# Decoder of two layers: the attention line of head pairs, with PSUM dealt anew between maxima and scores

## Chip, cores and metric

The program runs on one core of one Trainium2 chip, as one launch. The metric is the device time of an execution in microseconds (us), lower is better.

## What is computed

The reference is a decoder of two layers on x of 8 x 256 tokens by 128 features, with a context of the same size. Each of its six sublayers is followed by a layer norm of the sum with its input. Five stages of the kernel are attention with 16 heads of 8 features; what they share, cut to the core:

```python
q, k, v = split_heads(x @ Wq.T), split_heads(x @ Wk.T), split_heads(x @ Wv.T)
scores = einsum('bhqd,bhkd->bhqk', q, k) / sqrt(8)      # + a bias or a mask, by stage
attn = softmax(scores, axis=-1)
out = einsum('bhqk,bhkd->bhqd', attn, v)                # then out @ Wo.T in three of them
x = _layernorm(x + out)
```

The stages in order: **a0**, self-attention with rotary positions, 8 batches of 256 x 256 scores; **x0**, causal attention to the context with a linear bias; **f0**, causal attention among tokens that a router selects, 4 pairs of batches of 128 x 128 scores; **a1**, self-attention with a learned Gaussian bias, 8 batches; **x1**, attention to the context under an integer mask, 8 batches. Between them lie projections, layer norms, a gated layer after f0, and at the end a top-2 mixture of eight experts.

## The kernel before

It is written in Bass: each engine (PE = TensorE, DVE = VectorE, ACT = ScalarE, POOL = GpSimd, SP for the DMA queue) has its own instruction stream, and semaphores join them. No scheduler moves anything.

`Core` (tensor, scalar, vector, gpsimd, sync) is one attention stage. A batch, or a pair of selected batches in f0, is an **item**. Its 16 heads are 8 **pairs** u = 0..7, one head in rows 0 to 63 of the arrays Q6 and K6, the other in rows 64 to 127. Queries and keys stand there as six bf16 parts of each fp32 number. Each head is computed twice:

- **Maxima** (L413): queries on the partitions, 62 rows of contraction. DVE takes the negated row maxima from PSUM into MS (L574). After four pairs, a **half**, POOL splits them in two bf16 parts (L639, L640), PE turns them (L466, `turn_m`), ACT copies them to MT (L537), and SP writes them by DMA into rows 62, 63 and 126, 127 of Q6 (L684), against rows of ones in K6.
- **Scores** (L420): keys on the partitions, 64 rows of contraction, so that the row maximum is already subtracted. ACT takes the exponential from PSUM into PT (L550), and PE multiplies it with the values and a column of ones, in fp32, four heads side by side in 32 columns each (L480, `values`: one call for four heads, a **group**). ACT copies the result to OT (L529, `evacuate`), PE turns it (L493, `turn_context`), DVE divides by the sum (L589, L590, `context`).

Where a stage has a bias that is no extra row (x0, f0, x1), one more matmul with the identity adds it to each bank of maxima and of scores (L429).

PSUM has eight banks of 2 KB a partition. Before: banks 0 to 3 hold scores, two banks a pair and two pairs in turn; bank 4 holds the maxima of one head of the pair and bank 5 those of the other; bank 6 the products with the values; bank 7 what is turned.

`steps` walks j = 0..nb+1: in turn j the maxima are those of item j (`bm`), the scores those of item j-1 (`be`), and the end of item j-2 (`bc`) follows. Within a turn, `heads` gives for each pair u two phases a = 0, 1: in a phase the maxima of head a and the scores of head 1-a alternate matmul by matmul, so that two run side by side in the two halves of the rows. Only item j's maxima run in the first turn, so the scores follow eight pairs behind.

```python
if bm:
    after(pe, self.mx_done, H * bm.no + 2 * u + a - 1)
```

is the wait of a phase for the maxima bank, and `after(pe, self.exp_done, be.no * 8 + u - 1)` the wait for the score banks. `Post` puts pieces of the next projection and layer norm (T, C, P, A, M, N) into the last two turns, at the places in PLACES.

Of the kernel before, what the change touches and what calls it, by code (L numbers as in the profile page):

```python
# [333 lines left out]
class Item:  # L334
# [3 lines left out]
    def __init__(self, core, no, feat):  # L338
        self.core, self.no = core, no
        self.par = no % 2  # L340
        self.buf, self.use = no % NBUF, no // NBUF
        self.feat = feat


class Core:
# [3 lines left out]
    def __init__(self, g, nb, nqt, causal=False, bias=None, extra=None, xrows=0):  # L349
        assert nb % NBUF == 0  # L350
# [6 lines left out]
        self.tail = None  # L357

        self.st_ready = g.shared_sem("core_st_ready", 8 * nb)
        self.exp_done = g.shared_sem("core_exp_done", 8 * nb)  # L360
        self.mx_ready = g.shared_sem("core_mx_ready", H * nb)
        self.mx_done = g.shared_sem("core_mx_done", H * nb)
        self.mb_ready = g.shared_sem("core_mb_ready", 2 * nb)
        self.mt_ready = g.shared_sem("core_mt_ready", 2 * nb)
        self.mts_done = g.shared_sem("core_mts_done", 2 * nb)
        self.pv_done = g.shared_sem("core_pv_done", 4 * nb)
        self.ot_done = g.shared_sem("core_ot_done", 4 * nb)
        self.va_ready = g.shared_sem("core_va_ready", nb)
        self.cxt_ready = g.shared_sem("core_cxt_ready", nqt * nb)
        self.cx_done = g.shared_sem("core_cx_done", nqt * nb)  # L370
        self.chain = g.shared_sem("core_chain", nqt * nb)
        self.m_chain = g.shared_sem("core_m_chain", 2 * nb)
        self.joined = g.shared_sem("core_joined", 2 * nb if causal else 0)
        self.feat = [g.shared_sem(f"core_feat{i}", 16 * sum(self.loads(n) for n in range(i, nb, NBUF))) for i in range(NBUF)]
        self.m_in = [[g.shared_sem(f"core_m_in{i}{h}", 32 * nb // NBUF) for h in range(2)] for i in range(NBUF)]
        self.items = []
        for n in range(nb):
            loads = sum(self.loads(i) for i in range(n % NBUF, n + 1, NBUF))
            self.items.append(Item(self, n, 16 * loads))
# [1968 lines left out]
```

## Time and profile before

| | us |
|---|---|
| median of 3 executions | 1121.19 |
| lowest, highest | 1118.40, 1122.68 |
| the profiled execution | 1118.82 |
| its span, first to last instruction | 1117.0 |
| PE busy | 823.5 (74%) |
| DVE busy | 628.2 (56%) |
| ACT busy | 519.7 (47%) |
| mean granted TensorE clock | 0.823 |

The profiled execution takes 1.8 us more than its span. A busy PE is pipelined and its ends are modelled, so its share says little; the stages have different limits, and each is read by itself. The attention lines run from about 62 to 193 (a0), 220 to 360 (x0), 424 to 486 (f0), 572 to 704 (a1) and 731 to 911 us (x1); the experts follow to the end. A granted clock of 1.00 is 2.4 GHz, one of 0.50 is 1.2 GHz.

### The profile page before, as it was taken

To read this page: it belongs to the slowest core of one execution; us is meant where nothing else is said; L and a number is where in the kernel's file an instruction comes from. 1 tells how busy PE (TensorE), PEld (TensorE's weight loads), DVE (VectorE), ACT (ScalarE), POOL (GpSimd) and SP (SyncE) were. 2 spreads that over 40 slices of the span, in tenths; PEclk is the share of its full clock that TensorE was granted. 3 is DMA by queue.
4 is the path that set the end of the run, shared out by engine and by line. 5 is a ranking of instruction groups with operands and counts; after the bars stand their busy time and mean duration, and the time that the engine had idled before them with its cause. 6 is when DMAs were issued, how large, how long until landed. Compare 5 with 4: busy or idle time off the path is not lost.

```text
span 1117.0 us, 20492 instructions
## 1 busy us (share of the span) xinstructions
PE 823.5 (74%) x7236; PEld 457.0 (41%) x7237; DVE 628.2 (56%) x1590; ACT 519.7 (47%) x867; POOL 182.3 (16%) x312
## 2 busy tenths in 40 slices
PE   6167777489997546965847777489999962999970
PEld 3013334224443332433513334213333442999970
DVE  3287774466674733326257774446666435555567
ACT  2237776435555321313617776405555531666630
POOL 3421110100110020000501110210000006403214
PEclk9659999569998765558759999759999975999985
DMA  5842205332101022000522210142120051212212
GB/s 160 230 131 64 59 6 170 96 95 59 57 5 72 28 61 70 2 1 4 168 58 64 64 34 2 40 114 63 31 58 2 2 226 45 74 48 67 66 39 70
DMA packets 75657, 75.56 MB, mean 68 GB/s; under 512 B 21473, under 2 KB 65249, under 8 KB 74801
## 3 DMA queue, kind: packets, MB, share of 16 engines
q1 hardware_dynamic: 72400, 64.10, 20.9%
q0 software_dynamic: 3168, 10.29, 2.8%
q8 instruction: 55, 0.90, 0.4%
q14 instruction: 34, 0.27, 0.1%
HBM read 50.66 MB, written 23.13 MB: 66 GB/s over the span
## 4 chain that ended last, share of the span: by engine, by line
PE 61%; DVE 14%; issue 7%; SPq 5%; DMA 5%; POOL 4%; ACT 4%; POOLq 0%; ACTq 0%; DVEq 0%
PE PS L413 12%; PE PS L429 12%; PE PS L480 11%; PE PS L1611 7%; DVE MS L574 7%; PE PS L493 4%; PE PS L1621 3%; SPq L666 3%; PE PS L420 2%; PE PS L827 1%; PE PS L173 1%; POOL experts_x L1522 1%; ACT X L858 1%; DMA rows_k<-parts 1%; DMA BIG<-MT 1%
## 5 line engine op out<-in xcount | busy, mean ns | idle before, releaser
L574 DVE TENSOR_REDUCE MS<-PS 128x2 f32<-128x512 f32 (+2 forms) x576 | 341.2, 615 | 163.3 <-PE PS L429 120.5
L550 ACT ACTIVATE BIG<-PS 128x1024 f32<-128x1024 f32 (+2 forms) x288 | 259.9, 906 | 218.7 <-PE PS L429 157.2
L413 PE MATMUL PS<-BIG 62*128 62x256 bf16 (+1 forms) x1088 | 216.5, 287 | 131.0 <-DVE MS L574 56.6
L420 PE MATMUL PS<-BIG 64*128 64x256 bf16 (+1 forms) x1088 | 198.2, 274 | 0.5 <-DMA BIG<-MT 0.5
L413 PEld LDWEIGHTS PS<-BIG 62*128 62x128 bf16 x1088 | 70.3, 96 | 280.9 <-issue 189.0
L480 PE MATMUL PS<-BIG,VA 128*32 128x256 f32 (+1 forms) x2176 | 143.7, 377 | 3.5 <-ACT OT L529 3.5
L1611 PE MATMUL PS<-OT,VA 128*128 128x128 f32 x736 | 96.2, 278 | 0.4 <-ACT OT L1668 0.4
L1611 PEld LDWEIGHTS PS<-OT,VA 128*128 128x128 f32 x736 | 91.0, 195 | 0.6 <-ACT OT L1668 0.6
L480 PEld LDWEIGHTS PS<-BIG,VA 128*32 128x32 f32 x2176 | 62.4, 111 | 50.9 <-issue 29.9
L639 POOL CAST MB<-MS 128x16 bf16<-128x16 f32 (+1 forms) x72 | 14.1, 196 | 413.7 <-DVE MS L574 323.6
L589 DVE RECIPROCAL rsum<-PS 128x16 f32<-128x16 f32 x68 | 17.5, 257 | 110.3 <-PE PS L493 110.3
L300 POOL TENSOR_TENSOR parts<-rbuf,parts 128x512 bf16<-128x512 f32 x34 | 40.0, 1185 | 226.9 <-ACT parts L225 226.8
L420 PEld LDWEIGHTS PS<-BIG 64*128 64x128 bf16 x1088 | 66.9, 95 | 11.8 <-issue 5.5
L1663 ACT COPY VA<-BIG 128x1024 f32 x46 | 48.1, 1046 | 42.0 <-PE PS L1611 40.6
L1702 DVE SCALAR_TENSOR_TENSOR turn<-fbuf,PS 128x512 f32<-128x512 f32 x46 | 31.6, 687 | 55.4 <-ACT fbuf L1678 55.4
L537 ACT COPY MT<-PS 16x256 bf16<-16x256 bf16 (+1 forms) x72 | 24.5, 341 | 80.8 <-PE PS L466 65.9
L529 ACT COPY OT<-PS 128x256 f32<-128x256 f32 (+1 forms) x144 | 51.1, 355 | 16.3 <-PE PS L480 16.1
L493 PE MATMUL PS<-ident,OT 128*128 128x128 f32 x272 | 47.1, 299 | 15.7 <-issue 12.9
L429 PE MATMUL PS<-mask_q,ident_bf 128*128 128x512 bf16 x128 | 53.8, 421 | 0.0
L871 PE MATMUL PS<-ident,X 128*128 128x128 f32 x80 | 20.1, 401 | 40.5 <-ACT X L858 35.0
L1621 PE MATMUL PS<-BIG,rbuf 128*128 x368 | 49.1, 276 | 0.8 <-DVE Y L1716 0.8
L429 PE MATMUL PS<-mask_k,ident_bf 128*128 128x512 bf16 x128 | 49.2, 384 | 0.0
(218 smaller groups left out, 1092.3 us busy)
## 6 DMA issues: line engine op xcount, KB each, us to landing
rows_q<-parts SPq DMA_DIRECT2D x32, 192.0 KB, 2.3
rows_k<-parts SPq DMA_DIRECT2D x32, 192.0 KB, 2.2
BIG<-rows_q SPq DMA_DIRECT2D x64, 96.0 KB
BIG<-rows_k SPq DMA_DIRECT2D x64, 96.0 KB
BIG<-in_ex_w SPq DMA_DIRECT2D x3, 2048.0 KB, 12.0
BIG<-rows_q SPq DMA_DIRECT2D x64, 64.0 KB
BIG<-rows_k SPq DMA_DIRECT2D x64, 64.0 KB
OT<-experts_x SPq DMA_DIRECT2D x46, 64.0 KB, 1.8
```

The costliest lines, as they stand in the source:

```text
L300: nc.gpsimd.tensor_tensor(self.part(m, 2), g.rbuf[m % 2][:, :], self.part(m, 1), ALU.subtract).then_inc(self.s3_ready.sem, 1)
L413: return nc.tensor.matmul(g.bank[4 + a][:, first:first + kw], g.Q6[b.buf][rows, u, qt * P:(qt + 1) * P], g.K6[b.buf][rows, u, 0:kw], start ...
L420: return nc.tensor.matmul(g.bank[2 * (u % 2) + a][:, self.offset[kt]:self.offset[kt] + n], g.K6[b.buf][rows, u, kt * P:(kt + 1) * P], g.Q6 ...
L429: return nc.tensor.matmul(self.biased(bank), g.ident_bf[:, :], bias, start=False, stop=True)
L480: last = nc.tensor.matmul(g.bank[6][PVW * hh:PVW * hh + PVW, lo:lo + n], g.VA[b.par][:, kt, 8 * (hh % 2) + 2 * grp + hh // 2, :], g.PT[grp ...
L493: last = nc.tensor.transpose(g.bank[7][:, grp * P:(grp + 1) * P], g.OT[b.par][:, grp, qt * P:(qt + 1) * P], g.ident[:, :])
L529: nc.scalar.copy(g.OT[b.par][:, grp, 0:w], g.bank[6][:, 0:w])\
L550: nc.scalar.activation(g.PT[grp % 2][:, 2 * (u % 2):2 * (u % 2) + 2, 0:self.width], g.bank2[u % 2][:, :, 0:self.width], ACT.Exp, scale=SCALE)\
L574: nc.vector.tensor_reduce(g.MS[:, 0:n, a, u], g.bank[4 + a][:, 0:n * w].rearrange("p (n k) -> p n k", n=n), axis=AX_X, op=ALU.max, negate= ...
L1611: last = nc.tensor.matmul(g.bank[2 * a + b.par][:, f * P:(f + 1) * P], self.wb[b.par][:, a, f * P:(f + 1) * P], self.xt[b.par], start=True ...
L1621: last = nc.tensor.matmul(g.bank[6][:, 0:D], self.hid[b.par][:, f * P:(f + 1) * P], self.w3[:, bass.ds(e, 1), f, :].rearrange("p e d -> p ...
L1663: nc.scalar.copy(self.wb[b.par], self.w12[:, :, bass.ds(self.expert(nc.scalar, b), 1), :] .rearrange("p a e f -> p a (e f)"))
```

## The change

A class `Line` takes over the five engine streams from `Core`, with one count of steps for all stages. A step is one pair: maxima of pair `step`, scores of pair `step - LAG`, and LAG is 10.

- PSUM: banks 0 and 1 hold the scores, one for each head of the pair; banks 2 to 5 the maxima, two banks a pair and two pairs in turn. Banks 6 and 7 stay.
- Maxima: one reduction over both banks of a pair (288 instructions in place of 576), and one semaphore step a pair. A pair waits for the reduction two pairs before.
- Scores: one exponential a head (576 in place of 288), one semaphore step a head. A head's scores wait for the exponential of the same head of the pair before.
- `values` of a group comes in two parts, kt = 0 and kt = 1, each between the two phases of a step: kt = 0 at odd, kt = 1 at even score pairs. `turn_context` comes in two halves of two transposes each, in two steps.
- `evacuate` and the exponentials stand in this order in a step of ACT. On SP, the six key loads of an item stand after the maxima rows of the item two before, the query loads ahead of them. `Post`'s places are steps after the last maxima: the moments (M0) now stand at step 4.
- The semaphores are no longer per stage. The matmuls, their operands and the copies are the same.

The core of the diff:

```diff
+        for step in range(8 * first, 8 * end + self.TAIL):
+            yield step, inside(step, 8), inside(step - self.LAG, 8)
...
+        k, n = divmod(step - self.LAG - 14, 8)
+        b = self.item(items, k)
+        qt, half = {0: (0, 0), 1: (0, 1), 3: (1, 0), 4: (1, 1)}.get(n, (2, 0))
+        return (b, qt, half) if b and qt < b.core.nqt else (None, 0, 0)
...
+        k, n = divmod(step - 2, 8)
+        return (self.item(items, k - 1), 1) if n == 0 else (self.item(items, k), 0) if n == 4 else (None, 0)
...
-            return nc.tensor.matmul(g.bank[4 + a][:, first:first + kw], g.Q6[b.buf][rows, u, qt * P:(qt + 1) * P],
...
+            return nc.tensor.matmul(g.bank[2 + 2 * (u % 2) + a][:, first:first + kw], g.Q6[b.buf][rows, u, qt * P:(qt + 1) * P],
...
-            return nc.tensor.matmul(g.bank[2 * (u % 2) + a][:, self.offset[kt]:self.offset[kt] + n],
...
+            return nc.tensor.matmul(g.bank[a][:, core.offset[kt]:core.offset[kt] + n],
...
-        def phase(bm, be, u, a):
-
-            if bm:
-                after(pe, self.mx_done, H * bm.no + 2 * u + a - 1)
-            for i in range(nqt):
...
+        def phase(step, bm, be, a):
+
+            u, v = step % 8, (step - self.LAG) % 8
+            if bm and a == 0:
+                after(pe, self.mx_done, step - 1)
+            if be:
+                after(pe, self.exp_done, 2 * (step - self.LAG) + a - 1)
+            for i in range(2):
+                if bm and i < bm.core.nqt:
+                    mx = maxima(bm, u, a, bm.core.nqt - 1 - i, bm.core.bias is None or i == 0)
+                if be and i < be.core.nqt:
+                    st = scores(be, v, 1 - a, i, be.core.bias is None or i == 0)
...
+            if bm and a == 1:
                 mx.then_inc(self.mx_ready.sem, 1)
-            if be and a == 1:
+            if be:
                 st.then_inc(self.st_ready.sem, 1)
...
+            b, grp = self.group(items, n), n % 4
...
+                pe.wait_ge(*self.exp_done.at(4 * n + 4))
+            lo, w = core.queries[kt]
+            for hh in range(4):
+                last = nc.tensor.matmul(
+                    g.bank[6][PVW * hh:PVW * hh + PVW, lo:lo + w],
+                    g.VA[b.par][:, kt, 8 * (hh % 2) + 2 * grp + hh // 2, :],
+                    g.PT[grp % 2][:, hh, core.offset[kt]:core.offset[kt] + w],
+                    start=kt == 0, stop=kt == core.nqt - 1)
+            if kt == core.nqt - 1:
+                last.then_inc(self.pv_done.sem, 1)
...
+            if half == 0:
...
+            for grp in (2 * half, 2 * half + 1):
+                last = nc.tensor.transpose(g.bank[7][:, grp * P:(grp + 1) * P], g.OT[b.par][:, grp, qt * P:(qt + 1) * P],
+                                           g.ident[:, :])
+            if half == 1:
+                last.then_inc(self.cxt_ready.sem, 1)
+                self.bank7_read = self.cx_done.at(b.cx + qt + 1)
...
+        for step, bm, be in self.steps(items):
...
+            phase(step, bm, be, 0)
+            grp, kt = divmod(step - self.LAG - 3, 2)
+            values(grp, kt)
+            phase(step, bm, be, 1)
+            b, half = self.maxima_of(items, step)
+            if b:
+                turn_m(b, half)
+            b, qt, half = self.turns_of(items, step)
+            if b:
+                turn_context(b, qt, half)
+            if tail:
+                tail.run("tensor", pe, step)
+
...
-        def evacuate(b, grp):
-            act.wait_ge(*self.pv_done.at(b.no * 4 + grp + 1))
...
+            act.wait_ge(*self.pv_done.at(n + 1))
...
+            nc.scalar.copy(g.OT[b.par][:, grp, 0:w], g.bank[6][:, 0:w]).then_inc(self.ot_done.sem, 1)
...
+        def exponential(b, v):
+            if v % 2 == 0:
+                after(act, self.pv_done, v // 2 - 1)
+            w = b.core.width
+            for n, a in enumerate((1, 0)):
+                act.wait_ge(*self.st_ready.at(2 * v + n + 1))
+                nc.scalar.activation(g.PT[v // 2 % 2][:, 2 * (v % 2) + a, 0:w], g.bank[a][:, 0:w], ACT.Exp, scale=SCALE)\
+                  .then_inc(self.exp_done.sem, 1)
...
+            if v % 2 == 0:
+                evacuate(v // 2 - 2)
+            if be:
+                exponential(be, v)
...
-            n, w = self.mx_blocks, P if self.causal else nqt * P
-            for a in range(2):
-                dve.wait_ge(*self.mx_ready.at(H * b.no + 2 * u + a + 1))
-                nc.vector.tensor_reduce(g.MS[:, 0:n, a, u], g.bank[4 + a][:, 0:n * w].rearrange("p (n k) -> p n k", n=n),
-                                        axis=AX_X, op=ALU.max, negate=True).then_inc(self.mx_done.sem, 1)
+            dve.wait_ge(*self.mx_ready.at(step + 1))
+            nc.vector.tensor_reduce(g.MS[:, 0:n, :, u].rearrange("p n a -> p a n"),
+                                    g.bank2[1 + u % 2][:, :, 0:n * w].rearrange("p a (n k) -> p a n k", n=n),
+                                    axis=AX_X, op=ALU.max, negate=True).then_inc(self.mx_done.sem, 1)
...
+        for step, bm, be in self.steps(items):
+            if bm:
+                maxima(bm, step)
+                if bm.core.causal and step % 4 == 3:
+                    join(bm, step % 8 // 4)
+            b, qt, half = self.turns_of(items, step)
+            if b and half == 1:
+                context(b, qt)
+            if tail:
...
+        for b in items:
+            parts_of_m(b, 0)
+            value_rows(b)
+            parts_of_m(b, 1)
...
+    def sync(self, sp, items, rows):
...
+        for step, bm, be in self.steps(items):
+            b, half = self.maxima_of(items, step)
+            if b:
+                m_rows(b, half)
+            k, n = divmod(step, 8)
+            if n == 4:
+                b = self.item(items, k + 2)
+                if b:
+                    self.load(sp, b, rows, "qx")
+            if n == 0 and k > items[0].k:
+                b = self.item(items, k + 1)
+                if b:
+                    self.load(sp, b, rows, "k")
...
-    PLACES = {(0, 0): "T0 C0", (0, 1): "P0 T1 C1", (0, 2): "A0 P1 T2 C2", (0, 3): "A1 P2 M0", (1, 0): "A2", (1, 3): "N0 N1",
+    PLACES = {0: "T0 C0", 1: "P0 T1 C1", 2: "A0 P1", 4: "A1 M0", 5: "T2 C2", 6: "P2", 7: "A2", 12: "N0 N1",
...
-        self.bank2 = [PS[:, 2 * i:2 * i + 2, :] for i in range(2)]
+        self.bank2 = [PS[:, 2 * i:2 * i + 2, :] for i in range(3)]
```

The order on **PE** in a0, before: the second phase of pair 3, then a whole group of values and a whole context (L413 maxima, L420 scores, L480 values, L493 contexts).

```order
L413 MATMUL PS<-BIG 128x256 [waits core_mx_done]
L420 MATMUL PS<-BIG 128x256
L413 MATMUL PS<-BIG 128x256
L420 MATMUL PS<-BIG 128x256
L480 MATMUL PS<-BIG,VA 32x256 [waits core_ot_done,core_exp_done]
L480 MATMUL PS<-BIG,VA 32x256 x7
L493 MATMUL PS<-ident,OT 128x128 [waits core_ot_done,core_cx_done,core_mts_done]
L493 MATMUL PS<-ident,OT 128x128 x3
```

The same place in the changed kernel, one step of an odd score pair (L461 maxima, L468 scores, L525 values, L540 contexts): the first phase, half a group of values, the second phase, half a context.

```order
L461 MATMUL PS<-BIG 128x256 [waits core_exp_done,core_mx_done]
L468 MATMUL PS<-BIG 128x256
L461 MATMUL PS<-BIG 128x256
L468 MATMUL PS<-BIG 128x256
L525 MATMUL PS<-BIG,VA 32x256 [waits core_ot_done,core_exp_done]
L525 MATMUL PS<-BIG,VA 32x256 x3
L461 MATMUL PS<-BIG 128x256 [waits core_exp_done]
L468 MATMUL PS<-BIG 128x256
L461 MATMUL PS<-BIG 128x256
L468 MATMUL PS<-BIG 128x256
L540 MATMUL PS<-ident,OT 128x128 x2
```

The values and the context are cut in two, and half of the values stands between the phases. In an even step that half is kt = 1, whose last matmul is what `core_pv_done` counts.

The order on **ACT** in a0, before: a group's copy (L529), two exponentials of two heads each (L550), the copy of turned maxima (L537).

```order
L529 COPY OT<-PS 128x256 [waits core_cxt_ready,core_pv_done]
L550 ACTIVATE BIG<-PS 128x1024 [waits core_pv_done,core_st_ready]
L550 ACTIVATE BIG<-PS 128x1024 [waits core_st_ready]
L537 COPY MT<-PS 16x256 [waits core_m_in30,core_mt_ready]
L529 COPY OT<-PS 128x256 [waits core_pv_done]
```

The changed kernel at this place: the copy (L578), the two exponentials of an even pair (L586), the copy of turned maxima (L595), the two of an odd pair, the next copy.

```order
L578 COPY OT<-PS 128x256 [waits core_cxt_ready,core_pv_done]
L586 ACTIVATE BIG<-PS 128x512 [waits core_st_ready,core_pv_done]
L586 ACTIVATE BIG<-PS 128x512 [waits core_st_ready]
L595 COPY MT<-PS 16x256 [waits core_m_in30,core_mt_ready]
L586 ACTIVATE BIG<-PS 128x512 [waits core_st_ready] x2
L578 COPY OT<-PS 128x256 [waits core_pv_done]
```

Twice as many exponentials of half the width stand there, and the copy at the head of an even step waits for the half of values that PE issues in the same step.

## Rows read from the trace of the kernel before

**Rows 1.** Stretches: length, busy us (x) of PE, PEld, DVE, ACT, POOL, PEclk, DMA share, GB/s.

```profile
93.40:149.68 56.28, 42.65 (x564) 20.53 (x560) 44.31 (x80) 39.87 (x57) 5.77 (x20) 1.00 0.24 58
258.27:331.27 73.00, 71.53 (x865) 33.09 (x861) 51.32 (x110) 41.76 (x71) 7.22 (x25) 1.00 0.15 44
731.47:749.03 17.56, 17.56 (x50) 3.81 (x50) 10.39 (x15) 0.36 (x1) 0.42 (x2) 0.50 0.56 131
776.19:871.92 95.73, 95.73 (x864) 32.62 (x860) 61.75 (x100) 50.28 (x71) 7.20 (x25) 1.00 0.12 33
452.86:465.14 12.28, 12.28 (x110) 5.50 (x102) 5.15 (x18) 4.41 (x15) 1.17 (x6) 0.50 0.01 2
```

**Rows 2.** Timeline of x1, PE: start us, us, engine line op out<-in xcount [idle <-releaser].

```profile
757.56 1.07 PE L480 MATMUL PS<-BIG,VA 128*32 128x256 f32 x16
758.57 0.28 PE L413 MATMUL PS<-BIG 62*128 62x256 bf16 x1
...
759.43 0.28 PE L413 MATMUL PS<-BIG 62*128 62x256 bf16 x1
...
762.02 1.07 PE L480 MATMUL PS<-BIG,VA 128*32 128x256 f32 x16
762.90 0.28 PE L466 MATMUL PS<-ident_bf,MB 128*16 128x128 bf16 x2
```

**Rows 3.** Timeline of x0, PE.

```profile
242.46 0.28 PE L413 MATMUL PS<-BIG 62*128 62x256 bf16 x1
...
243.06 0.86 PE L480 MATMUL PS<-BIG,VA 128*32 128x256 f32 x16
```

**Rows 4.** Timeline of a0, PE.

```profile
110.07 0.28 PE L413 MATMUL PS<-BIG 62*128 62x256 bf16 x1
...
110.39 1.07 PE L480 MATMUL PS<-BIG,VA 128*32 128x256 f32 x16
...
113.58 1.07 PE L480 MATMUL PS<-BIG,VA 128*32 128x256 f32 x16
114.58 0.66 PE L493 MATMUL PS<-ident,OT 128*128 128x128 f32 x4
...
115.17 0.28 PE L413 MATMUL PS<-BIG 62*128 62x256 bf16 x1
```

**Rows 5.** Timeline of a0, ACT and DVE.

```profile
110.53 1.02 ACT L550 ACTIVATE BIG<-PS 128x1024 f32<-128x1024 f32 x1 [0.70 <-PE PS L420]
...
111.86 0.36 ACT L529 COPY OT<-PS 128x256 f32<-128x256 f32 x1
111.91 2.54 DVE L574 TENSOR_REDUCE MS<-PS 128x2 f32<-128x512 f32 x4 [0.65 <-PE PS L413]
...
112.17 1.02 ACT L550 ACTIVATE BIG<-PS 128x1024 f32<-128x1024 f32 x1
...
114.72 0.37 ACT L529 COPY OT<-PS 128x256 f32<-128x256 f32 x1
```

**Rows 6.** Groups by line and shape: busy us, mean ns | idle us before <-releaser.

```profile
L574 DVE TENSOR_REDUCE MS<-PS 128x2 f32<-128x512 f32 x384 | 251.4, 688 | 86.3 <-PE PS L429 48.5 <-PE PS L413 34.0 <-POOL MB L640 0.6
...
L550 ACT ACTIVATE BIG<-PS 128x768 f32<-128x768 f32 x64 | 51.8, 810 | 54.6 <-PE PS L429 54.6
...
L1678 ACT ACTIVATE fbuf<-PS 128x512 f32<-128x512 f32 x46 | 27.4, 597 | 6.2 <-PE PS L1611 3.2
```

**Rows 7.** Timeline after the last maxima of a0.

```profile
178.67 0.38 ACT L529 COPY OT<-PS 128x256 f32<-128x256 f32 x1
...
179.19 1.07 PE L480 MATMUL PS<-BIG,VA 128*32 128x256 f32 x16 [0.49 <-ACT OT L529]
```

**Rows 8.** Timeline, PE: the first scores of x0.

```profile
236.46 0.37 PE L413 MATMUL PS<-BIG 62*128 62x256 bf16 x1 [3.72 <-DMA BIG<-MT]
```

**Rows 9.** Timeline, PE: the first scores of f0.

```profile
435.44 0.26 PE L413 MATMUL PS<-BIG 62*128 62x128 bf16 x1 [4.02 <-DMA BIG<-MT]
```

**Rows 10.** Timeline, PE: the last context of x0.

```profile
359.13 1.09 PE L493 MATMUL PS<-ident,OT 128*128 128x128 f32 x4 [5.22 <-issue]
```

More of the change, by code:

```diff
@@ L356, in __init__ @@
         self.mx_blocks = 3 if causal else nqt
[L357 to L379, printed above, removed]
+        self.items = g.line.add(self)
     def loads(self, no):
         return 12 + (2 if self.xrows else 0) + (2 if self.extra is not None and no < NBUF else 0)
-    def steps(self, body):
-        for j in range(self.nb + 2):
-            body(j, *(self.items[j - lag] if 0 <= j - lag < self.nb else None for lag in range(3)))
     def bias_for(self, b, transposed):
@@ L416, in scores @@
[L416 to L422 removed]
+            core, rows = b.core, slice(64 * a, 64 * a + MROW)
+            first = P if core.causal and qt == 1 else qt * core.nqt * P
@@ L446, in phase, with turn_m @@
                 mx.then_inc(self.mx_ready.sem, 1)
-            if be and a == 1:
+            if be:
                 st.then_inc(self.st_ready.sem, 1)
-        def heads(bm, be, u):
-            if bm and u == 0:
+        def turn_m(b, half):
+            pe.wait_ge(*self.mb_ready.at(2 * b.k + half + 1))
+            if self.bank7_read:
+                pe.wait_ge(*self.bank7_read)
+            for qt in range(b.core.nqt):
+                last = nc.tensor.transpose(g.aux_bf[0:16, qt * P:(qt + 1) * P], g.MB[half][:, qt, :], g.ident_bf[:, :])
+            last.then_inc(self.mt_ready.sem, 1)
+            self.bank7_read = self.mts_done.at(2 * b.k + half + 1)
@@ L453, in heads @@
+        self.bank7_read = None
+        for step, bm, be in self.steps(items):
+            if bm and step % 8 == 0:
                 pe.wait_ge(*self.feat[bm.buf].at(bm.feat))
             if be:
-                if u % 4 == 0:
-                    pe.wait_ge(*self.m_in[be.buf][u // 4].at((be.use + 1) * 32))
-                after(pe, self.exp_done, be.no * 8 + u - 1)
-            phase(bm, be, u, 0)
-            phase(bm, be, u, 1)
-        def turn_m(b, half):
-            after(pe, self.cx_done, self.turned)
-            pe.wait_ge(*self.mb_ready.at(b.no * 2 + half + 1))
-            for qt in range(nqt):
-                last = nc.tensor.transpose(g.aux_bf[0:16, qt * P:(qt + 1) * P], g.MB[half][:, qt, :], g.ident_bf[:, :])
-            last.then_inc(self.mt_ready.sem, 1)
-            self.m_turned += 1
@@ L487, in turn_context @@
-        def turn_context(b, qt):
-            after(pe, self.mts_done, self.m_turned)
-            after(pe, self.cx_done, self.turned)
-            pe.wait_ge(*self.ot_done.at(b.no * 4 + 4))
-            for grp in range(4):
-                last = nc.tensor.transpose(g.bank[7][:, grp * P:(grp + 1) * P], g.OT[b.par][:, grp, qt * P:(qt + 1) * P],
-                                           g.ident[:, :])
-            last.then_inc(self.cxt_ready.sem, 1)
-            self.turned += 1
-        self.m_turned = self.turned = 0
@@ L780, in run @@
         if place != "after":
-            place = (place[0] - self.core.nb, place[1])
+            place -= 8 * self.core.items[-1].k + 8
         pieces = {"T": self.turn, "C": self.copy, "P": self.project, "A": self.add,
```

409 lines of the change are left out of this document (193 added, 216 removed).

## Prediction

> **What bounds the kernel now.** I read first the windows over whole items of each stage [rows 1], since the page's shares are means over stages with different limits. In a0 an item takes 56.28 / 4 = 14.07 us; PE is busy 42.65 of the 56.28 and DVE 44.31, so none is full, and a ring of waits sets the pace. a1 has the same pitch. In x0 an item takes 73.00 / 5 = 14.60 us and in x1 95.73 / 5 = 19.15 us, and there PE is busy 71.53 of 73.00 and all of the stretch. f0 takes 12.28 us an item at a granted clock of 0.50, PE busy throughout. Then the timelines, for which ring it is in a0: DVE reduces four banks in 2.54 us, idle 0.65 us before them for a PE matmul [rows 5], and PE's phases wait for the maxima bank just reduced. That wait, at every phase, is what four banks of maxima take away. Last, the edges: x0's and f0's first scores stood 3.72 and 4.02 us for the maxima rows' DMA [rows 8, 9], and x0's last context waited 5.22 us with no releaser named, behind DVE's moments [rows 10].
>
> **What takes its place.** With two banks of scores, phase 0 of a step must wait for the exponential of that head in the step before; with half of the values between the phases, an even step's exponentials stand behind a copy that waits for the values of the same step. So a double step is a chain through PE, ACT and back. Its parts:
> - Values on PE: sixteen matmuls are followed by a maxima matmul after 1.01 us and by a transpose after 0.88 us [rows 2], so a half is 0.44 us, and the change to a phase 0.13 us more: 0.57 us.
> - Phase: 0.32 us in a0 [rows 4], 0.60 in x0 [rows 3], 0.86 in x1 [rows 2].
> - Start of the values to the copy's start: 1.14 us for a group (113.58 to 114.72) [rows 4, 5], less 0.44: 0.70.
> - Copy to exponential: 111.86 to 112.17 is 0.31 us; phase start to exponential is 0.46 us (110.07 to 110.53) [rows 4, 5].
> - Exponential of 512 columns: no row has it from PSUM to PT. 1024 columns take 1.02 us [rows 5], 768 take 0.81 and an ACT read of 512 elsewhere takes 0.597 [rows 6]; the two lines give 0.60, and 0.49 for 384. Bounds: half of 1.02 (0.51) and 0.81.
> - End of an ACT instruction to PE's start: 178.67 + 0.38 to 179.19 is about 0.11 us with the rounding [rows 7].
> - Context: 0.59 us for four transposes [rows 4], so 0.37 for two, if about 0.15 of it is the change of operands and comes again. Bounds 0.30 and 0.59.
>
> **a0 and a1.** Even step: 0.32 + 0.70 + 0.31 + 0.60 + 0.11 = 2.04 us. Odd step: 0.46 + 0.60 + 0.11 = 1.17, or 1.55 in the two that carry half a context. An item: 4 x 2.04 + 2 x 1.17 + 2 x 1.55, plus 0.3 for ACT's two copies of turned maxima, is 13.9 us against 14.07: the ring of DVE goes, and one of nearly the same length comes. With LAG 10, 54 of 64 steps carry both kinds of work (before 56), that is 6.75 items: -0.8 us. Edges: ten maxima steps in place of eight, bound by DVE. The merged reduction has no row: two single ones are 1.38 us [rows 6], four in a row go at 2.54 / 4 = 0.635 a piece, so 1.27 a pair [rows 5]; I take 1.2, between 1.07 (0.69 and half of 0.76) and 1.38. So 12.0 - 11.0 = +1.0, two full steps of 1.76 less, -3.5, and two more score steps without maxima at the mean of the chain, 2 x 1.6 = +3.2. Each stage: -0.1 us.
>
> **x1.** PE has no idle time, so each added piece counts. Values per item: eight halves at 0.57 = 4.60 for four groups of 0.88 to 1.00, together 3.76: +0.84. Contexts: 4 x 0.37 for 2 x 0.59: +0.3. The chain of an even step, 0.86 + 0.70 + 0.31 + 0.60 + 0.11 = 2.58, is 0.08 longer than PE's own work in the two steps with turned maxima: +0.16. Together +1.3, by 6.75 items +8.9 us. Edges: a maxima step at the low clock is 17.56 / 8 = 2.19 us [rows 1]; two of these and two score steps of 1.6 for two full ones of 2.39: +2.8. Sum +11.7.
>
> **x0.** Even step 0.60 + 0.49 + 0.31 + 0.49 + 0.11 = 2.00 (values and exponential of the narrower causal form), odd step 0.60 + 0.57 + 0.60 = 1.77 on PE, twice with 0.37: 15.8 us against 14.60, by 6.75 +8.3 us. Edges: the maxima rows now stand ahead of the key loads on SP, and the wait of 3.72 [rows 8] covers two more maxima steps of 1.38, which leaves -0.96; two full steps less, -3.65; two score steps more, +3.5, less about half of the 5.22 [rows 10], since the moments now stand at step 4, which leaves +1.0 of the score steps. Sum +4.7.
>
> **f0.** Only one key block, so kt = 1 is empty and no half is added; the split contexts and exponentials add about 0.4 an item at half clock: +1.1. The wait of 4.02 [rows 9] covers two more maxima steps of at most an eighth of an item, 12.28 / 8 = 1.54, and leaves -0.9; two full steps less: -3.1; two score steps of about 1.2, an estimate from 1.54 less the maxima: +2.4. Sum -0.5.
>
> **POOL, SP, DVE.** POOL's parts and SP's DMAs are as many as before. DVE issues 288 instructions fewer, which is worth nothing once it isn't the ring; the 0.65 us gap [rows 5] covers it, and if the chain above were shorter than DVE's 1.2 a step it would count.
>
> **Sum.** -0.1 - 0.1 + 11.7 + 4.7 - 0.5 = +15.7 us on the profiled 1118.82, 1134.5; the median of the runs is 2.4 us higher, so about **1136 us**. Its own range, from the bounds of the exponential (two of them in the chain of a double step: 0.09 us less each takes 4 x 2 x 0.09 x 6.75 = 4.9 us from a0 and as much from a1), and of the context (0.59 in place of 0.37 adds 4 x 0.22 x 6.75 = 5.9 us in x1 and as much in x0, where PE is full): 1125 to 1146.
>
> **A rule against this change.** The rows show 0.13 us between values and a phase where the next matmul reads other rows [rows 2], and the sum uses that. The Trainium skill, "TensorEngine Tiling (Array Packing)", section "Key Properties", says that a change of the tiling mode drains TensorE, and values in four tiles of 32 columns between phases in two row halves are such changes, now twice as many; the trace agrees that there is a price. Sixteen values matmuls take 1.07 us to their last end [rows 2] and the next one of a phase starts 0.06 us before that; taking the whole pipeline, an estimate by that rule, 0.2 us for each of the eight halves in place of 0.13 would add some 0.6 us an item in x1 and 2 to 4 us in all.
>
> **Rivals.**
> - **The chain does not bind (faster).** Place: ACT's copy at the head of an even step in a0 and a1. If the values' half ends so early beside the phases that the exponential starts with its scores, a double step falls to what DVE needs, 2 x 1.2 + its share of divisions, 2.75 us instead of 3.5, an item to 11.0: (14.07 - 11.0) x 13.5 = -41 us, about 1095; half way is about 1115. It decides at a double step under 3.4 us. For it: PE and DVE are each idle a quarter of the stretch [rows 1]. Against: 0.70 and 0.31 are rows of instructions that stay. The Trainium skill, "VectorE: DVE Perf Modes", section "The DRAIN you can't avoid", states that a DVE instruction starts only when the one before has emptied the pipe, which would favour one instruction a pair; the row of four at 0.635 apiece where one takes 0.69 shows little such gap here. Chance 0.14.
> - **Splitting costs nothing on PE (no change).** If values and contexts in halves run as fast as whole, and x0's chain hides behind PE, the 8.9 and 8.3 us go: about 1119. For it: transposes follow values in 0.88. Against: 1.01 where a phase follows. Chance 0.19.
> - **Late maxima rows (slower still).** Scores wait for the DMA that SP issues. If each half of an item comes some 0.5 us late in 27 items of the four long stages, that is +25 us, about 1161. For it: [rows 8, 9] show such waits at the edges. Against: LAG 10 gives two steps, over 3 us, more. Chance 0.15.
> - Forecast: 0.52.
>
> **Numbers.** The range leaves out the far ends of the first and third rivals: 1110 to 1156. A measurement here tells some 0.5%, 5.6 us, from no change, 1115.6 to 1126.8. Faster: the first rival and a little of the second, 0.18. Same: the rest of the second and the forecast's low end, 0.22. Slower: 0.60.
>
> **What would show it.** Windows of 14.0 us an item in a0 and a1, 15.8 in x0, 20.5 in x1, 12.7 in f0. One group of 288 reductions, about 1.2 us at full width. In even steps ACT's copies wait for PE's values and PE's phases for ACT; DVE's idle time grows. The clock stays. A double step in a0 under 3.4 us, or x1 still at 19.2 an item, would make it wrong.

## The result, and the profile after

The changed kernel takes 1122.86 us (median of 20 executions), the kernel before 1119.53 (20 executions): a ratio of 1.0034, 95% interval 1.0017 to 1.005. That is a small loss, a fifth of the one forecast (about 16 us), and inside the 0.5% that the prediction called no change. The profiled execution's span grew from 1117.0 to 1118.7 us.

Busy time by engine, from the page of the changed kernel, and its costliest groups on DVE, ACT and PE:

```profile
PE 855.2 (76%) x7236; PEld 436.8 (39%) x7237; DVE 595.9 (53%) x1302; ACT 545.7 (49%) x1155; POOL 181.3 (16%) x312
...
L619 DVE TENSOR_REDUCE MS<-PS 128x4 f32<-128x1024 f32 (+2 forms) x288 | 307.7, 1076 | 236.2 <-PE PS L478 180.7
L586 ACT ACTIVATE BIG<-PS 128x512 f32<-128x512 f32 (+2 forms) x576 | 298.5, 540 | 147.1 <-PE PS L478 112.5
L461 PE MATMUL PS<-BIG 62*128 62x256 bf16 (+1 forms) x1088 | 213.9, 291 | 109.1 <-ACT BIG L586 25.9
```

DVE has 288 instructions less and 32 us less work, ACT 288 more and 26 us more, and PE, with the same 7236 matmuls, 32 us more busy time. PE's phases now wait for the exponential (L461, 25.9 us in all).

The windows of the changed kernel, two items of a0, x0 and x1, one of f0, and the ten maxima steps at the start of x1 (columns as in [rows 1]):

```profile
106.50:133.97 27.47, 23.84 (x282) 8.57 (x281) 21.31 (x25) 20.90 (x45) 2.77 (x10) 1.00 0.21 60
270.92:301.86 30.94, 29.61 (x345) 12.41 (x344) 18.16 (x28) 17.92 (x45) 2.78 (x10) 1.00 0.19 54
799.12:839.02 39.90, 39.85 (x345) 12.67 (x344) 21.76 (x25) 21.97 (x45) 2.90 (x10) 1.00 0.14 42
450.18:462.58 12.40, 12.40 (x104) 5.39 (x103) 4.04 (x10) 5.43 (x22) 1.12 (x5) 0.50 0.01 3
726.62:748.51 21.89, 21.89 (x64) 4.74 (x64) 11.03 (x9) 0.36 (x1) 1.38 (x5) 0.50 0.38 104
```

An item takes 13.73 us in a0 (and a1), 15.47 in x0, 19.95 in x1 and 12.40 in f0. Before it was 14.07, 14.60, 19.15 and 12.28 by [rows 1]. The windows here run from one transpose of maxima to that of an item later; taken so, the full items before come out at the same 14.07, 14.60 and 19.15.

The new chain can be read off the timelines of PE and ACT in a0 (matmuls of maxima, values, context):

```profile
107.33 0.27 PE L461 MATMUL PS<-BIG 62*128 62x256 bf16 x1 [0.55 <-ACT BIG L586]
...
108.53 0.27 PE L461 MATMUL PS<-BIG 62*128 62x256 bf16 x1
...
108.85 0.64 PE L525 MATMUL PS<-BIG,VA 128*32 128x256 f32 x8
...
109.42 0.28 PE L461 MATMUL PS<-BIG 62*128 62x256 bf16 x1
...
110.58 0.27 PE L461 MATMUL PS<-BIG 62*128 62x256 bf16 x1 [0.39 <-ACT BIG L586]
...
112.17 0.28 PE L461 MATMUL PS<-BIG 62*128 62x256 bf16 x1
```

```profile
109.56 0.37 ACT L578 COPY OT<-PS 128x256 f32<-128x256 f32 x1 [0.28 <-PE PS L525]
109.83 1.77 ACT L586 ACTIVATE BIG<-PS 128x512 f32<-128x512 f32 x3
```

An even step runs from 108.53 to 110.58: phase 0.32, values to the copy's start 0.71, copy to exponential 0.27, exponential and the way back 0.75. That is 2.05 us where the prediction summed 2.04. The odd step without a context runs from 107.33 to 108.53, 1.20 us (predicted 1.17), the one with a context from 110.58 to 112.17, 1.59 (predicted 1.55). But neither at 108.53 nor at 112.17 does PE wait: these steps are as long as PE's own work (0.32 + 0.57 + 0.31 is 1.20), and not as long as a chain through ACT, so that their sums came out close by luck. Four even steps, two odd ones and two with a context make 13.78 of the measured 13.73 us; the 0.3 that the prediction added for ACT's copies of turned maxima isn't there.

The table shows where the 1.7 us between the profiled spans come from, by part of a stage, beside the prediction's terms. "Full" runs from the first scores to the last maxima, "fill" is before it, "drain" after it to the end of the last context:

| us | fill: before, after, change (forecast) | full | drain | stage (forecast) |
|---|---|---|---|---|
| a0 | 25.03, 24.52, -0.5 (+1.0) | 96.29, 91.05, -5.2 (-4.3) | 22.70, 26.02, +3.3 (+3.2) | -2.4 (-0.1) |
| x0 | 16.32, 15.50, -0.8 (-1.0) | 100.81, 103.05, +2.2 (+4.6) | 22.94, 23.47, +0.5 (+1.0) | +1.9 (+4.7) |
| f0 | 11.52, 10.59, -0.9 (-0.9) | 35.48, 31.63, -3.9 (-2.0) | 14.34, 16.71, +2.4 (+2.4) | -2.4 (-0.5) |
| a1 | 11.56, 11.10, -0.5 (+1.0) | 96.46, 93.00, -3.5 (-4.3) | 23.26, 26.47, +3.2 (+3.2) | -0.7 (-0.1) |
| x1 | 17.57, 21.89, +4.3 (+4.4) | 131.08, 132.26, +1.2 (+4.1) | 29.27, 31.99, +2.7 (+3.2) | +8.2 (+11.7) |

With -2.9 us between the stages and at both ends (forecast 0) this is +1.7 (forecast +15.7). No single term was off by more than 3 us.

### The profile page after: what moved, and what is told of

Read it like the earlier page. It is cut to its first block, busy times and chain, and to the rows that moved or that the text cites. A ratio compares the mean times of both kernels' runs of the same rounds, so it can differ in the third digit from the quotient of the medians.

```text
span 1118.7 us, 20452 instructions
## 1 busy us (share of the span) xinstructions
PE 855.2 (76%) x7236; PEld 436.8 (39%) x7237; DVE 595.9 (53%) x1302; ACT 545.7 (49%) x1155; POOL 181.3 (16%) x312
## 4 chain that ended last, share of the span: by engine, by line
PE 62%; DVE 11%; ACT 8%; issue 7%; POOL 4%; DMA 4%; SPq 3%; POOLq 0%; ACTq 0%; DVEq 0%
PE PS L525 13%; PE PS L461 12%; PE PS L478 12%; PE PS L1653 7%; ACT BIG L586 4%; PE PS L1663 3%; PE PS L468 3%; DVE MS L619 3%; PE PS L540 2%; SPq L707 2%; PE PS L173 1%; POOL experts_x L1564 1%; PE PS L869 1%; ACT X L900 1%; DMA rows_k<-parts 1%
## 5 line engine op out<-in xcount | busy, mean ns | idle before, releaser
L619 DVE TENSOR_REDUCE MS<-PS 128x4 f32<-128x1024 f32 (+2 forms) x288 | 307.7, 1076 | 236.2 <-PE PS L478 180.7
L586 ACT ACTIVATE BIG<-PS 128x512 f32<-128x512 f32 (+2 forms) x576 | 298.5, 540 | 147.1 <-PE PS L478 112.5
L461 PE MATMUL PS<-BIG 62*128 62x256 bf16 (+1 forms) x1088 | 213.9, 291 | 109.1 <-ACT BIG L586 25.9
L468 PE MATMUL PS<-BIG 64*128 64x256 bf16 (+1 forms) x1088 | 211.0, 275 | 2.6 <-ACT BIG L586 2.4
L461 PEld LDWEIGHTS PS<-BIG 62*128 62x128 bf16 x1088 | 66.4, 97 | 272.0 <-issue 189.5
L525 PE MATMUL PS<-BIG,VA 128*32 128x256 f32 (+1 forms) x2176 | 169.5, 385 | 2.5 <-ACT OT L578 2.5
L578 ACT COPY OT<-PS 128x256 f32<-128x256 f32 (+1 forms) x144 | 51.9, 360 | 78.8 <-PE PS L525 78.6
L468 PEld LDWEIGHTS PS<-BIG 64*128 64x128 bf16 x1088 | 64.5, 96 | 30.1 <-issue 15.3
L525 PEld LDWEIGHTS PS<-BIG,VA 128*32 128x32 f32 x2176 | 43.9, 110 | 71.1 <-issue 54.6
L595 ACT COPY MT<-PS 16x256 bf16<-16x256 bf16 (+1 forms) x72 | 24.2, 336 | 81.3 <-PE PS L507 66.2
L540 PE MATMUL PS<-ident,OT 128*128 128x128 f32 x272 | 57.0, 299 | 7.2 <-DVE CX L637 6.8
```

Of the source, the lines that this page charges most:

```text
L461: return nc.tensor.matmul(g.bank[2 + 2 * (u % 2) + a][:, first:first + kw], g.Q6[b.buf][rows, u, qt * P:(qt + 1) * P], g.K6[b.buf][rows, u ...
L468: return nc.tensor.matmul(g.bank[a][:, core.offset[kt]:core.offset[kt] + n], g.K6[b.buf][rows, v, kt * P:(kt + 1) * P], g.Q6[b.buf][rows, ...
L525: last = nc.tensor.matmul(g.bank[6][PVW * hh:PVW * hh + PVW, lo:lo + w], g.VA[b.par][:, kt, 8 * (hh % 2) + 2 * grp + hh // 2, :], g.PT[grp ...
L540: last = nc.tensor.transpose(g.bank[7][:, grp * P:(grp + 1) * P], g.OT[b.par][:, grp, qt * P:(qt + 1) * P], g.ident[:, :])
L578: nc.scalar.copy(g.OT[b.par][:, grp, 0:w], g.bank[6][:, 0:w]).then_inc(self.ot_done.sem, 1)
L586: nc.scalar.activation(g.PT[v // 2 % 2][:, 2 * (v % 2) + a, 0:w], g.bank[a][:, 0:w], ACT.Exp, scale=SCALE)\
```

## The experiments

Each is an edit of the changed kernel, beside which the before-kernel ran on the same chip. The ratio is to the kernel before; "against the change" compares medians with its 1122.86.

### Where the values stand: whole_odd, whole_even

```diff
-            if not b or kt >= b.core.nqt:
+            if not b or kt != min(0, b.core.nqt - 1):     (whole_even: min(1, ...))
                 return
...
-            lo, w = core.queries[kt]
-            for hh in range(4):
+            for kt in range(core.nqt):
+                lo, w = core.queries[kt]
+                for hh in range(4):
```

> The values of a group are not split: all eight matmuls (both key blocks) stand between the phases of the odd step, where the first half stood. Chain theory (an even step's copy and exponentials wait for the values half that PE issues in the same step): in a0 and a1 that wait goes, but the odd step gets longer, a double step about 3.35 us in place of 3.43, an item 13.4 in place of 13.73; in x1 PE does four groups of 1.0 instead of eight halves of 0.57, an item 19.3 in place of 19.95; x0 15.1 in place of 15.47. In all about -12 us against the changed kernel. Rival (the two score banks alone set the pace, the copy's place is nothing): a0 and a1 gain nothing or lose 0.4 an item, in all about -4 to 0.

> All of a group's values stand between the phases of the even step, where the second half stood. Chain theory: the chain of the even step grows by the first half, 0.44 us: a0 and a1 13.73 + 4 x 0.43 = 15.4 us an item, x0 16.7, x1 19.7 (PE saves 0.6, the chain takes 0.3 back); about +30 us against the changed kernel. Rival (the copy's place is nothing): the same work as the run before, so the same time, -4 to 0 us.

whole_odd took 1105.86 us, ratio 0.9877 (0.9827 to 0.9926), -17 us against the change; whole_even 1128.95, ratio 1.0087 (1.0056 to 1.0117), +6 us. Windows of two items of a0, x0, x1, first of whole_odd, then of whole_even:

```profile
108.01:135.58 27.57, 22.85 (x283) 9.54 (x281) 21.04 (x25) 20.44 (x45) 2.78 (x10) 1.00 0.21 60
270.93:299.60 28.67, 28.29 (x345) 13.03 (x344) 17.91 (x29) 18.55 (x45) 2.78 (x10) 1.00 0.19 58
...
789.71:827.90 38.19, 37.24 (x339) 13.26 (x345) 21.76 (x25) 22.17 (x44) 2.77 (x10) 1.00 0.15 44
```

```profile
111.03:140.34 29.31, 23.85 (x283) 9.46 (x281) 21.41 (x24) 19.96 (x45) 2.90 (x10) 1.00 0.19 56
280.45:310.88 30.43, 28.79 (x346) 13.35 (x345) 18.17 (x29) 17.89 (x45) 2.90 (x10) 1.00 0.19 55
...
810.55:849.37 38.82, 37.80 (x340) 13.49 (x345) 21.77 (x25) 21.96 (x45) 2.90 (x10) 1.00 0.14 43
```

The two hold the same instructions; only the place differs, and with it a0's item is 13.78 or 14.65 us, x0's 14.34 or 15.22, x1's 19.10 or 19.41. So the rival by which the copy's place is nothing falls. PE's timeline of whole_even shows the longer chain, its even step going from 120.38 to 122.86, 2.48 us, which is 2.05 and the other half's 0.43:

```profile
120.38 0.27 PE L461 MATMUL PS<-BIG 62*128 62x256 bf16 x1
...
120.71 1.07 PE L525 MATMUL PS<-BIG,VA 128*32 128x256 f32 x16
...
122.86 0.27 PE L461 MATMUL PS<-BIG 62*128 62x256 bf16 x1 [0.39 <-ACT BIG L585]
```

Its item grew by 0.92 us, not the 1.7 expected: four such double steps of 2.48 and about 1.18 us are the 14.65. That is less than expected, since two of the four double steps carried half a context in the odd step and had taken 3.63 us already; in whole_even that context hides in the longer wait. In whole_odd a0 kept its time (13.4 was expected): the odd step is longer by the same half, and once an item the transposes of maxima stand for DVE's context, 0.86 us where the changed kernel has 0.39:

```profile
115.53 0.27 PE L507 MATMUL PS<-ident_bf,MB 128*16 128x128 bf16 x2 [0.86 <-DVE CX L636]
```

x0 and x1 gained more than expected, and x1 is back at its pace before the change. So in x1 all of the +0.80 us an item, and in x0 more than all of the +0.87, hangs on the split and on where the second half stands.

### Two reductions a pair: two_red

```diff
-            nc.vector.tensor_reduce(g.MS[:, 0:n, :, u].rearrange("p n a -> p a n"),
...
+            for a in range(2):
+                last = nc.vector.tensor_reduce(g.MS[:, 0:n, a, u],
...
+            last.then_inc(self.mx_done.sem, 1)
```

> The banks stay as changed, but DVE reduces a pair in two instructions of one head each, with one semaphore step after the second. Chain theory: DVE is off the path in full steps, items stay at 13.7, 15.5 and 19.95; only the ten maxima steps at a stage's start run at 1.3 to 1.4 us in place of 1.2, +1 to +2 us in each of a0, x0 and a1, in all +3 to +6 us. Rival (DVE still sets the pace in a0 and a1, so the merged reduction is what the change gains by): 0.15 us a step and more, +10 us in each of a0 and a1, +20 us in all.

1122.01 us, ratio 1.0027 (0.9997 to 1.0057), -1 us against the change; items 13.73, 15.48 and 19.96 as there. The merged reduction is worth nothing that can be told in this kernel.

### The lag: lag9

```diff
-    LAG = 10
+    LAG = 9
```

The turned contexts keep their steps.

> The scores follow nine pairs behind the maxima instead of ten (the turned contexts stay at their absolute steps). If LAG 10 pays for the way of the maxima rows: from the transpose to the second DMA's issue is 2.2 us in the changed kernel's trace, and with some 2 us to land about 4.2 us; two steps between cover 3.4 in a0 and a1, so PE waits 0.8 us twice an item there, 15.3 in place of 13.73, and little in x0 and x1; about +15 to +25 us less 4 for the edges. Rival (two steps cover it, as in the kernel before): items as now, each stage one maxima step and one score step shorter at its edges and one full step longer, -3 to -5 us in all.

1131.75 us, ratio 1.0099 (1.0078 to 1.0119), +9 us against the change. Items 14.21, 15.89 and 20.37, each 0.42 to 0.48 longer. But inside the full steps PE never waits for the maxima rows' DMA; only first scores do, those of f0 for 2.69 us, against 1.54 with LAG 10 and 4.02 before [rows 9], those of a0 and a1 for 1.01 and 0.85, against nothing. So both expectations miss. In a0 the timeline shows the reason: with an odd LAG the transposes of maxima fall in odd score steps, where nothing hides them, and the double step with them takes 126.26 - 122.78 = 3.48 us in place of 3.25:

```profile
122.78 0.27 PE L461 MATMUL PS<-BIG 62*128 62x256 bf16 x1 [0.76 <-ACT BIG L586]
...
124.00 0.28 PE L507 MATMUL PS<-ident_bf,MB 128*16 128x128 bf16 x2
...
126.26 0.27 PE L461 MATMUL PS<-BIG 62*128 62x256 bf16 x1 [0.76 <-ACT BIG L586]
```

In x0 and x1 it is PE's wait for exponentials that grew: over two items each of lag9's trace it stands 2.2 us (x0) and 0.9 (x1) in front of L461, against 1.3 and nothing in the changed kernel, that is 0.4 us an item in both. An even step keeps the length of its chain when the transposes leave it, and the odd step gets longer by them.

### Whole contexts: ctx_whole

```diff
-            for grp in (2 * half, 2 * half + 1):
+            if half == 0: return
+            for grp in range(4):
```

> Contexts are turned whole (four transposes in the step of the second half). The prediction priced the split at +0.3 us an item, so by it x1 falls from 19.95 to 19.65 and x0 from 15.47 to 15.2, -4 us in all. Rival (the split of a context costs nothing, since the two switches are no dearer than one phase's end that overlaps them): all items as now, 0 +- 1 us; in a0 and a1 the DVE's context comes at the same step in both cases.

1118.23 us, ratio 0.9981 (0.996 to 1.0003), -5 us against the change. But x0 stayed at 15.48 and x1 rose to 20.10, while a0 and a1 fell to 13.56. The term it tests, +0.3 us an item for the split in the stages where PE is full, has the wrong sign in x1. The timelines say what a context costs PE there. From the start of the phase before it to the next phase, first in the changed kernel (half a context), then in ctx_whole (a whole one):

```profile
810.82 0.28 PE L461 MATMUL PS<-BIG 62*128 62x256 bf16 x1
...
811.58 0.38 PE L540 MATMUL PS<-ident,OT 128*128 128x128 f32 x2
811.90 0.28 PE L461 MATMUL PS<-BIG 62*128 62x256 bf16 x1
```

```profile
810.41 0.28 PE L461 MATMUL PS<-BIG 62*128 62x256 bf16 x1
...
811.18 0.60 PE L541 MATMUL PS<-ident,OT 128*128 128x128 f32 x4
811.71 0.28 PE L461 MATMUL PS<-BIG 62*128 62x256 bf16 x1
```

The half takes 1.08 us and the whole 1.30; less a phase of 0.86 that is 0.22 for two transposes and 0.44 for four, so in x1 the split of a context costs PE nothing. And two of the four halves of an item fall in even steps, whose length of 2.58 us is the chain's. With whole contexts one even step has none, and waits for its exponential all the same:

```profile
821.47 0.27 PE L461 MATMUL PS<-BIG 62*128 62x256 bf16 x1 [0.22 <-ACT BIG L587]
```

### One exponential a pair: one_exp

```diff
-            for n, a in enumerate((1, 0)):
-                act.wait_ge(*self.st_ready.at(2 * v + n + 1))
...
+            act.wait_ge(*self.st_ready.at(2 * v + 2))
+            nc.scalar.activation(g.PT[v // 2 % 2][:, 2 * (v % 2):2 * (v % 2) + 2, 0:w], g.bank2[0][:, :, 0:w], ACT.Exp, scale=SCALE)\
```

> The exponential of a pair is one instruction over both score banks (1024 columns), as before the change, with the banks as changed. Chain theory: each step becomes a chain through both phases and the whole exponential: a0 and a1 0.89 + 0.46 + 1.02 + 0.11 = 2.48 us a step, 19.8 an item; x0 about 2.8 a step, 22.6 an item; x1 3.5 a step, 28 an item; about +190 us against the changed kernel. Rival (ACT and PE overlap otherwise, the split of the exponential only costs instructions): ACT saves 0.1 us a pair, no change or a few us less.

1531.62 us (one execution), +409 us against the change: the chain is there, and in all it costs twice the 190 us expected. Windows of two items of a0 and of x1:

```profile
140.35:195.81 55.46, 40.78 (x282) 10.63 (x280) 21.75 (x24) 20.32 (x28) 2.88 (x10) 0.50 0.10 30
...
1165.50:1223.74 58.24, 39.46 (x340) 12.90 (x345) 21.76 (x25) 20.31 (x28) 2.89 (x10) 1.00 0.10 29
```

In x1, at a granted clock of 1.00, an item takes 29.1 us where the chain gave 28. In a0 it takes 27.7 where the chain gave 19.8, and there the granted clock has fallen to 0.50. So the split of the exponential is what makes two banks of scores bearable.

### Values one step early: early, early_mixed

```diff
-            grp, kt = divmod(step - self.LAG - 3, 2)
+            grp, kt = divmod(step - self.LAG - 2, 2)
...
             for n, a in enumerate((1, 0)):
+                if v % 2 == 1 and n == 1:
+                    evacuate((v - 3) // 2)
...
-            if v % 2 == 0:
-                evacuate(v // 2 - 2)
```

The copy now stands between the two exponentials of the odd step. early_mixed adds: in x0 and x1 both halves at the odd step.

> The halves stay, one step earlier (first half in the even step right after the group's exponentials, second half in the odd step), and ACT's copy stands between the two exponentials of the odd step, so that no exponential waits for values of its own step. Chain theory: a double step in a0 and a1 becomes 0.89 + 1.17 + 0.89 = 2.95 us, an item 12.0 to 12.3 in place of 13.73; x0 15.3, x1 19.8; about -23 us against the changed kernel. Rival (ACT's load or the two score banks set the pace): a0 and a1 stay at 13.7, total within 5 us of the changed kernel.

> As the run with the values one step early and ACT's copy between the exponentials, and in x0 and x1, where PE is full, the values of a group whole in the odd step. a0 and a1 13.2 as in that run; x0 14.3 in place of 14.64, x1 19.1 in place of 19.65; -6 us against that run, about 1093. Rival (the split costs PE nothing once the chain is gone): the same time as that run.

early took 1099.56 us, ratio 0.9822 (0.9765 to 0.988), -23 us against the change as expected, but otherwise shared out: a0 and a1 13.20 (12.0 to 12.3 expected), x0 14.64, x1 19.65. early_mixed took 1094.49, ratio 0.9763 (0.9743 to 0.9783): x0 14.34 and x1 19.10, as expected. PE's timeline of early still shows the values waiting for an exponential, since the second phase of the odd step stands behind half of the values:

```profile
122.88 0.64 PE L525 MATMUL PS<-BIG,VA 128*32 128x256 f32 x8 [0.26 <-ACT BIG L588]
```

### Values behind both phases: late_values, late_ctx, late_whole

```diff
             phase(step, bm, be, 0)
-            values(grp, kt)
             phase(step, bm, be, 1)
+            values(grp, kt)
```

This is an edit of early_mixed. The copy then stands after both exponentials of the odd step. late_ctx moves the contexts to steps 7, 0, 3, 4; late_whole has whole groups in a0 and a1 too.

> As the last run (early values, halves in a0 and a1, whole groups in x0 and x1), but the values stand after both phases of a step and ACT's copy after both exponentials of the odd step. Chain theory: in a0 and a1 the second phase no longer stands behind a half of values, a double step's chain falls to about 2.65 us, below PE's own work of 16 x 0.32 + 8 x 0.57 + 4 x 0.37 + 2 x 0.24 = 11.6 us an item; so 11.8 to 12.2 in place of 13.20, x0 and x1 as before, about 1077. Rival (the waits of the transposes for DVE's context and ACT's load set the pace now): 13.2 stays, no change.

> As late_values, and the contexts of a batch at steps 7, 0, 3, 4 of eight in place of 0, 1, 3, 4, so that no transpose of maxima follows a context by one step. Theory: PE's waits of 0.3 to 0.4 us for DVE's context before the transposes go, 0.3 us an item in a0 and a1, -4 us against late_values. Rival: the wait only moves, no change.

> As late_ctx, with whole groups of values in a0 and a1 too, in the odd step after both phases. Theory: PE saves 4 x (2 x 0.57 - 1.0) = 0.56 us an item, the chain of a double step becomes 2.8 us: item 11.3 to 11.8, -3 to -5 us against late_ctx. Rival (the longer odd step lets ACT run dry): item 0.3 to 0.5 longer, +4 to +7 us.

late_values 1066.47 us, ratio 0.9514 (0.9489 to 0.9538); late_ctx 1062.17, ratio 0.9496 (0.9463 to 0.9528); late_whole 1088.08, ratio 0.969 (0.9647 to 0.9732). Windows of two items of a0 and x1 of late_ctx:

```profile
102.00:124.29 22.29, 22.27 (x284) 9.29 (x280) 20.73 (x25) 20.00 (x45) 2.81 (x10) 1.00 0.25 73
...
743.01:781.79 38.78, 38.78 (x345) 12.91 (x344) 21.75 (x25) 23.05 (x44) 2.79 (x10) 1.00 0.15 43
```

An item of a0 takes 11.15 us, PE is busy all of it, and no phase waits any more. The theory held, with more gain than expected from late_values in a0 and a1 (11.30 an item; 11.8 to 12.2 was expected), while x1, which was to stay at 19.10, rose to 19.39. The -4 us expected of late_ctx came in the medians, but not from where it was expected: the item fell by 0.15 us and not 0.3, which is 2 us in the two stages, and in the profiled execution the stretch between f0 and a1, where nothing was changed, was 5.7 us shorter. late_whole went its rival's way and three times as far, 12.57 us an item where 0.3 to 0.5 more was said. PE is busy 22.43 us of 25.14 there, against 22.27 of 22.29: whole groups save no PE time in this place, and in the odd step with all eight matmuls PE comes to wait for exponentials, 1.34 us an item.

late_ctx beats both kernels by 5%.

### Two reductions again: late_two_red

> As late_ctx, but DVE reduces a pair in two instructions. Theory: with the chain gone, DVE's load is next to PE's in a0 and a1 (eight reductions of 1.2 and two contexts of 0.65 us, 10.9 us of an item of 11.15), so that now the merged reduction counts: 8 x 2 x 0.64 to 8 x 1.38 and 1.3 give 11.6 to 12.3 us an item, +3 to +8 us in each of a0 and a1, +6 to +16 us against late_ctx. Rival (PE alone sets the pace there): as in the run of two reductions on the changed kernel, 0 to +3 us.

It ran on a chip on which the kernel before takes 1155.47 us: 1101.49, ratio 0.9511 (0.9478 to 0.9544), the same as late_ctx's within the intervals, and an item of a0 takes 11.15 us again. DVE's timelines say why, three merged reductions in late_ctx, six single ones in late_two_red:

```profile
133.97 3.60 DVE L623 TENSOR_REDUCE MS<-PS 128x4 f32<-128x1024 f32 x3
```

```profile
140.55 3.65 DVE L624 TENSOR_REDUCE MS<-PS 128x2 f32<-128x512 f32 x6
```

Back to back a merged one costs 1.20 us and two single ones 1.22. The expectation had priced two single ones at 1.28 to 1.38.

## Why the prediction was wrong

In short: the chain was foreseen rightly, the small terms around it were sized too dear, first of all the 0.37 us for half a context.

- **The mechanism in a0 and a1 was right, to 0.05 us a step.** The DVE ring went and a chain of nearly its length came; 13.73 us an item where 13.9 was summed. The odd steps are PE's work and not a chain, which changed their sum by 0.03.
- **The step that failed most: "so 0.37 for two" transposes of a context, in x0 and x1.** It took half of a context's 0.59 and a whole change of operands from a0 [rows 4]. In a0 it holds (1.59 - 1.20 = 0.39). In x1 it measured 0.22 (above), and in x0 0.21:

```profile
291.77 0.28 PE L461 MATMUL PS<-BIG 62*128 62x256 bf16 x1
...
292.27 0.38 PE L540 MATMUL PS<-ident,OT 128*128 128x128 f32 x2
292.58 0.28 PE L461 MATMUL PS<-BIG 62*128 62x256 bf16 x1
```

From phase to phase this is 0.81 us, with 0.60 of it the phase. In x0 and x1 a context follows a phase that ends on bias matmuls, and its first transpose starts 0.16 us before the last of these ends; in a0 it is 0.07.
- **x0's item, +1.22 forecast, +0.87 measured.** Its even step is 2.00 us (281.08 to 283.08) and its odd one 1.77, both as summed; the odd one with half a context is 1.98 and not 2.14. Two of these an item, over 6.75 items, are 2.2 of the 2.4 us that "full" was off. By the windows, PE's work grew by 0.50 us an item (14.31 to 14.81) and its waiting by 0.37 (0.29 to 0.66).
- **x1's item, +1.3 forecast, +0.80 measured, failed on the same term and was right on the values.** Halves of values cost 0.57 us each against 1.00 for a group, as written, and whole groups in the odd step take off 0.85 us an item where 0.84 had been added. "Contexts: 4 x 0.37 for 2 x 0.59: +0.3" is refuted: two halves lie in even steps, which last the chain's 2.58 us anyway, and two cost 0.23 in odd steps. Four even steps, two odd ones of 2.29 and two of 2.52 make 19.94. Over 6.75 items the 0.5 us are 3.4 us; "full" was off by 2.9.
- **Fill of a0 and a1, +1.0 forecast, -0.5 measured.** "Ten maxima steps, bound by DVE" at 1.2 us left out that PE waits only for the reduction two pairs before, so that the first scores of a0, at 72.22 us, stand behind nine reductions and not ten. And these follow each other at (10.26 - 1.23) / 8 = 1.13 us:

```profile
61.80 1.23 DVE L619 TENSOR_REDUCE MS<-PS 128x4 f32<-128x1024 f32 x1
...
62.95 10.26 DVE L619 TENSOR_REDUCE MS<-PS 128x4 f32<-128x1024 f32 x9
```

- **f0, -0.5 forecast, -2.4 measured.** "The split contexts and exponentials add about 0.4 an item" was +0.1. The two saved full steps are 3.1 of the 3.9 us of "full"; the rest is not traced.
- **Between the stages, 0 forecast, -2.9 measured.** In the runs here each of these stretches varies by 1 to 3 us with nothing changed in it (once by 5.7, in late_ctx), and their sum lies between 458 and 463 us in most, against 462.4 before and 459.5 here, so no cause is given.
- **All the costs were rounded up together.** Seven terms (the fills of a0 and a1, the full steps of a0, x0, f0 and x1, the stretches between), each 0.9 to 2.9 us too dear, made 14 us. The range of the forecast, 1125 to 1146, let only the exponential be cheaper; the cheap side of a context, 0.30, was named as a bound and left out. The median, 1122.86, is inside the whole range of 1110 to 1156, but the sign was given 0.60 and "same", which it was, 0.22. That it lies inside owes more to the far ends kept for the rivals than to the sum.
- **Rival 1 (the chain does not bind)** fell for the change as made. Its price is close to what the last variants reached, 11.15 us for a0's item where the rival had 11.0, but by luck: moving the copy's wait alone (early) gave 13.20, and at 11.15 it is PE that is full, not DVE as the rival had it.
- **Rival 2 (splitting costs nothing)** named 1119, and the median came out near it, but by luck: its condition is refuted by whole_odd, -17 us. **Rival 3 (late maxima rows)** showed no wait in any full step, not even with LAG 9.
- **The rule on tiling modes.** The trace agrees that a switch is paid: a half to the next phase takes 0.57 us, 2 x 0.57 - 1.00 = 0.14 a split, near the 0.13 of [rows 2] and below the 0.2 estimated from the rule. The Trainium skill, "TensorEngine Tiling (Array Packing)", section "Key Properties", names the drain on a change of mode and gives no figure for it.
- **The rule on DVE's drain.** The Trainium skill, "VectorE: DVE Perf Modes", section "The DRAIN you can't avoid", would have one instruction a pair be cheaper than two. Six single reductions in 3.65 us against three merged in 3.60 hardly bear that out, 0.02 us a pair.

## What to carry to other kernels

When a change takes a wait away, write out the chain that closes next, in steps of the program's own order, and price it from rows; here that gave the item's time to 3% in every stage. Then ask of each instruction in the new chain whether it must stand there: the change's idea was worth 5%, and lost it to half a group of values standing between two phases and to a copy standing ahead of two exponentials. In a sum of many small costs, the errors all go one way if each is rounded to the dear side; and a cost read in one stage need not hold in another, where other work stands in front of it.
